# Causal attention: order of whole-array units and maxima on TensorE

## The reference

```python
x = x + attn(layernorm(x), Wq, Wk, Wv)

q = einsum('bte,hed->bhtd', x, Wq); k = ...Wk; v = ...Wv
scores = einsum('bhtd,bhsd->bhts', q, k)
scores = where(causal, scores, -inf) / sqrt(256)
w = softmax(scores, axis=-1)
out = einsum('bhts,bhsd->bhtd', w, v)
```

## Time and profile before

| what | value |
|---|---|
| median of 3 runs | 4440.13 us (4440.07 to 4441.22) |
| span of the profiled execution | 4440.5 us |
| TensorE matmul busy | 4192.7 us, 94% |
| VectorE busy | 2790.9 us, 63% |
| ScalarE busy | 2654.5 us, 60% |
| GpSimd busy | 1452.8 us, 33% |
| maxima, reduction L648 | 738.3 us in 1280 instructions |

### The profile page before, as it was taken

One profiled execution on the slowest core, in us unless ns is written; L12 is line 12 of the kernel. 1 busy time (PEld: TensorE's weight loads), 2 busy tenths in 40 slices (PEclk: granted clock), 3 DMA queues, 4 the chain that ended last, 5 costly groups with the idle time before them and its releaser, 6 DMA issues. The chain is left out here.

```text
span 4440.5 us, 62548 instructions
## 1 busy us (share of the span) xinstructions
PE 4192.7 (94%) x22580; PEld 2203.7 (50%) x22580; DVE 2790.9 (63%) x5566; ACT 2654.5 (60%) x3193; POOL 1452.8 (33%) x1111
## 2 busy tenths in 40 slices
PE   7999999999978999999999999998899999999999
PEld 4444444544535565565565565555344444444443
DVE  6777777777748677676676645554455554555553
ACT  2555555555556454454454423444688888888888
POOL 3111111111125343343343322221354544545545
PEclk7999999999999999999999999999899999999999
DMA  7333433433210000000000001000766667667673
GB/s 176 89 94 74 102 74 81 95 96 80 60 56 1 0 1 1 1 1 1 1 1 1 1 8 26 1 1 1 166 143 161 152 143 164 149 153 162 141 162 90
DMA packets 145746, 322.79 MB, mean 73 GB/s; under 512 B 39296, under 2 KB 64272, under 8 KB 129056
## 3 DMA queue, kind: packets, MB, share of 16 engines
q1 hardware_dynamic: 137456, 310.88, 30.5%
q10 hardware_dynamic: 7920, 7.87, 0.6%
q0 software_dynamic: 64, 0.05, 0.0%
HBM read 237.93 MB, written 80.74 MB: 72 GB/s over the span
## 5 line engine op out<-in xcount | busy, mean ns | idle before, releaser
L2108 ACT ACTIVATE gelu_out<-hidden,b_col 128x1024 f32<-128x1024 f32 x1024 | 1084.4, 1112 | 164.6 <-PE hidden L2008 163.8
L648 DVE TENSOR_REDUCE maxima<-front 128x1 f32<-128x512 f32 (+3 forms) x1280 | 738.3, 631 | 170.7 <-PE front L458 97.2
L2090 POOL TENSOR_TENSOR combined<-combined,gated 128x512 f32<-128x512 f32 x480 | 619.6, 1291 | 666.9 <-DVE gated L2205 458.9
L550 ACT ACTIVATE probsT<-scoresT 128x1024 f32<-128x1024 f32 (+3 forms) x768 | 584.1, 811 | 306.1 <-PE scoresT L486 301.6
L1061 POOL TENSOR_TENSOR pair_sums<-sims 128x1024 f32<-128x1024 f32 x256 | 481.9, 1903 | 784.5 <-DVEq L1187 516.7
L2205 DVE SCALAR_TENSOR_TENSOR gated<-expert_out,b_col,gates_spread 128x512 f32<-128x512 f32 x480 | 360.1, 750 | 501.9 <-PE expert_out L2018 296.2
L2008 PE MATMUL hidden<-slice_stack,w_stack 128*128 128x512 f32 x2048 | 628.0, 428 | 15.0 <-ACT gelu_out L2108 15.0
L2018 PE MATMUL expert_out<-gelu_out,w_sb 128*32 128x512 f32 x4096 | 548.6, 608 | 24.9 <-DVE gated L2205 13.5
L2008 PEld LDWEIGHTS hidden<-slice_stack,w_stack 128*128 128x128 f32 x2048 | 352.4, 189 | 371.8 <-ACT gelu_out L2108 283.1
L399 POOL TENSOR_SCALAR_AFFINE_SELECT probsT<-probsT 128x512 f32<-128x512 f32 x256 | 163.3, 638 | 1075.4 <-ACT probsT L550 1075.4
L452 PE MATMUL front<-k_stack,q_stack 62*128 62x512 f32 (+3 forms) x1536 | 434.8, 427 | 34.6 <-DVE maxima L648 14.7
(11 more groups left out here) (203 smaller groups left out, 5663.0 us busy)
## 6 DMA issues: line engine op xcount, KB each, us to landing
gates_spread<-gate_scratch SPq DMA_DIRECT2D x512, 256.0 KB, 4.9
stack_scratch<-split_parts SPq DMA_DIRECT2D x192, 256.0 KB, 3.0
slice_stack<-slice_scratch SPq DMA_DIRECT2D x128, 256.0 KB, 8.1
q_stack<-stack_scratch SPq DMA_DIRECT2D x64, 384.0 KB, 6.2
k_stack<-stack_scratch SPq DMA_DIRECT2D x64, 384.0 KB, 9.2
slice_scratch<-slice_parts SPq DMA_DIRECT2D x32, 512.0 KB, 6.4
out_x<-x_tiles ACTq DMA_DIRECT2D x15, 512.0 KB, 4.8
x_tiles<-in_L_attn_x SPq DMA_DIRECT2D x7, 1024.0 KB, 12.3
```

What stands on the lines that cost most here:

```text
L550: nc.scalar.activation(PT[:, i % NPT, 2 * pr:2 * pr + 2, at:BANK], ST[pr][:, :, at:BANK], ACT.Exp, scale=SCALE).then_inc(probs_ready, 1)
L648: nc.vector.tensor_reduce(dst, F[k % 3][:, 0:parts * w].rearrange("p (a k) -> p a k", a=parts), AX.X, ALU.max)\
L2090: nc.gpsimd.tensor_tensor(CM[:, par, hc, :], CM[:, par, hc, :], Y[:, u % 2, :], ALU.add)\
L2108: nc.scalar.activation(GH[:, k % 4, :, :], HP[k % HPB][:, :, :], ACT.Gelu, bias=b1c[:, u % E:u % E + 1])\
```

## The change

The planner's second half is rewritten. Whole-array units that come due are no longer put in at once: they are collected in `late` and put in directly behind the next value piece (or the output transpose behind it), where the next piece is a score piece. Pairs of maxima are put in only where the next piece is a score piece, that is between the two score pieces of a group, or behind the value piece, its output transpose and the whole-array units; not ahead of a value piece. The transposes of the row maxima (`turn_after`) are collected in the same way. The load that is caught up with is computed as before, and the number and content of the units are the same.

```diff
-        whole = sum(pe_time(u) for u in pieces if u[0] in "sv")
-        rest, spent = [], 0.0
-        for u in pieces:
-            while spread and spread[0][0] * whole <= spent:
-                rest.append(spread.pop(0)[1])
-            rest.append(u)
-            if u[0] in "sv":
-                spent += pe_time(u)
-        rest += [u for _, u in spread]
-
...
-        whole, spent = sum(load_of(u) for u in rest), 0.0
-        all_pairs, done, k = sum(pair_load(p) for p in pairs), 0.0, 0
-        out = []
-        for u in rest:
+
+        out, late, k = [], [], 0
+        whole, at_whole = sum(pe_time(u) for u in pieces if u[0] in "sv"), 0.0
+        work = sum(load_of(u) for u in pieces) + sum(load_of(u) for _, u in spread)
+        all_pairs, done, spent = sum(pair_load(p) for p in pairs), 0.0, 0.0
+        for u, after in zip(pieces, pieces[1:] + [None]):
             out.append(u)
             spent += load_of(u)
-            while k < len(pairs) and (done + pair_load(pairs[k]) / 2) * whole <= spent * all_pairs:
-                out += pairs[k]
-                done += pair_load(pairs[k])
-                k += 1
-                out += [turn_after[k]] if k in turn_after else []
-        return out + [u for pair in pairs[k:] for u in pair]
+            at_whole += pe_time(u) if u[0] in "sv" else 0.0
+            if u[0] in "vo" and (after is None or after[0] == "s"):
+                while spread and spread[0][0] * whole <= at_whole:
+                    late.append(spread.pop(0)[1])
+                out += late
+                spent += sum(load_of(w) for w in late)
+                late = []
+            if after is None or after[0] == "s":
+                while k < len(pairs) and (done + pair_load(pairs[k]) / 2) * work <= spent * all_pairs:
+                    out += pairs[k]
+                    done += pair_load(pairs[k])
+                    k += 1
+                    late += [turn_after[k]] if k in turn_after else []
+        return out + late + [u for _, u in spread] + [u for pair in pairs[k:] for u in pair]
```

## The result

| | before | after |
|---|---|---|
| median | 4440.68 us (4440.07 to 4442.83) | 4618.66 us (4611.4 to 4634.23) |
| ratio | 1 | 1.0406, 95% interval 1.0387 to 1.0424 |
| span of the profiled execution | 4440.5 us | 4609.7 us |
| last value piece starts | 1279.3 us | 1451.9 us |

A forecast was written before the change was run, and what follows sets the result against it. The prediction took TensorE's own stream plus stalls from tile-form changes and three front banks emptied by VectorE as the bound. Terms -34 - 7 + 88 + 20 + 8 + 17 = +92 us gave 4532 us; range 4460 to 4600.

The forecast's parts named there:

- 1, fewer fragments: Attention on TensorE: 170 fewer row-tiled fragments save 34 us, 64 fewer whole-array ones save 7 us.
- Term 2: Attention's maxima: bunched pairs stall TensorE on three front banks VectorE must empty; +88 us, bounds +45 and +125.
- Term 3: Evacuations losing cover: maxima behind projections +20 us (bounds 0 to 30), o x x x +8 us (0 to 15).
- Term 4: Attention: idle stretches drop TensorE's clock to 1.2 GHz; 7 falls of 2.5 us, +17 us, bounds 0 and +78.
- the third rival: Attention: the clock falls at every long bunch of maxima pairs, +153 us in all, 4593 us; chance 0.11.
- The first (banks don't bind): Attention: fragments are saved and the front banks don't bind, so the kernel gets faster, 4399 us; chance 0.12.
- The second (later waits absorb earlier ones): Attention: TensorE's later waits absorb earlier ones, stalls grow by half, 88 becomes 44, about 4471 us; chance 0.12.
- the clock rival: Same as the third rival: the clock falls at every long bunch in attention, 4593 us; chance 0.11.

The follow-up runs named there:

- e7: Kernel after, with maxima matmuls of second and later pairs in fragments of three or more pairs issued three times; 4594.72 us, 1.0348 of before.
- e12: Kernel before with two front banks in use instead of three; 4753.09 us by one execution.
- e4: Kernel after with VectorE's reduction reading only the first 64 columns of each part; 4436.52 us, 0.9982 of before.
- e5: Kernel before with VectorE's reduction reading only the first 64 columns of each part; 4349.54 us, 0.9792 of before.

## Why the prediction was right or wrong

Step by step, from the trace of the kernel after, with fragments outside the half-clock stretches for the stalls:

| term | forecast | measured |
|---|---|---|
| 1, fewer fragments | -34 and -7 | -34 by the packed prices, not measured by itself; whole-array ones with term 3 about 0 |
| 2, stalls of bunched pairs, and 3, behind p | +88 and +20 | +138 |
| 3, o x x x | +8 | +8 to 15, cancels the -7 |
| 4, clock | +17 | +65 |
| sum | +92 | about +170 (172.6 by the last value piece) |

*What bounds, and the fragments.* Right. At the full clock a value piece takes 1.00 us whatever stands behind it, before and after, and two wide scores alone take 0.66 in both, as packed. No experiment shows the saving by itself, since none saved fragments and left the maxima alone.

*Term 2.* The mechanism and the unit price hold: M M s s behind a value piece stalls 1.00 us at the full clock (54 fragments; forecast 0.95), behind a lone projection 1.82 (forecast 0.95 + 0.8), M s M s 0.87 in the median (forecast 0.85). Mis-sized by 30 us together were the tails: M s M s has a mean of 1.03; three pairs stall 1.9 and not 1.2, since seven of the fifteen stand behind o t w, whose statistics and row-maxima parts are ahead of the reductions in VectorE's queue (2.85 us); and the fragments with one pair stall 0.18 and those with none 0.35 instead of 0.1, so that having fewer of them saved next to nothing. I priced each fragment as though it met an idle VectorE.

*Term 3.* The six places o x x x wait 1.7 to 4.3 us each for normalised x, 14.0 us in all, where I had 1.2 each. About half of the stall was there before in another form: x x o took 2.0 us and x x 1.3 us, six times each, where x x takes 0.59 when nothing holds it up.

*Term 4* is the step that failed most: the number of falls, not their price. I took 7 falls of 2.5 us; there were 29 against 3, and 65 us for 26 more is again 2.5 us each. It is seen best in the value pieces, which wait for nothing once they start: 375 of them took 324 us, where 374 took 303 before, so some 21 us are clock alone, and by the same comparison whole-array fragments give some 26 and row-tiled ones 18. In the prediction the third rival held what was missing as a size (every long bunch brings a fall: +78), with a chance of 0.11. As a mechanism it was half right: 13 of the 29 falls stand behind one of the 32 long bunches of the stage, and behind the others none came within 3.4 us. What I held against it, that the idle stretches are shorter than 1.35 us, didn't help: the longest idle stretch in the window from 641.0 us was 0.90 us. Falls also came where I hadn't looked: 10 of the 29 behind fragments with only two pairs, most of them behind a projection or on the narrow diagonal, and 4 behind o x x x; the last 2 are among the scores at the end of the stage. That these others are set off in the same way is likely but wasn't tested; e7 filled only the long bunches.

*Rivals.* The first (banks don't bind) is refuted by the result, by e12 and by e4 and e5. The second (later waits absorb earlier ones) didn't happen except that scores wait less on the exponentials, 31.6 instead of 68.0 us. The rule of the Trainium skill, TensorEngine Tiling (Array Packing), Key Properties, that a change of tiling mode drains the engine, comes into play some 230 times less here. The 0.2 us of a row-tiled fragment agree with it, though no run separates the drain from the first weight load. The rule of the same page, PSUM Bottleneck, that tiling doesn't speed up the emptying of PSUM, is the one that decided: VectorE's 0.68 us for each reduction is what e4 took away.

The range ended at 4600, the time is 4619. It took in the clock rival only up to 4600 and never that rival together with the upper bound of term 2 (+125), though both have the same cause: longer bunches stall more and let the clock fall more. Ends of terms with one cause belong together.

## What to carry to other kernels

Where several units share a few PSUM banks, what a reorder costs is read from one fragment: how soon the bank comes back (here 1.2 to 1.4 us, of which the reduction is 0.55 to 0.68) and what else TensorE has to do in that time; grouping work of one form to save switches (0.2 us each) takes that cover away. Price each stall by what stands ahead of it in the emptying engine's queue, not from idle. And stalls of a microsecond have a second price: count the stretches in which TensorE idles off and on, since each may bring some microseconds at 1.2 GHz.

## What the runs showed of the hardware

- The granted clock fell to 0.50, the 1.2 GHz level, at 644.4 us behind a stretch in which TensorE was still busy 2.37 of 3.40 us, and at 968.7 us behind one with 3.15 of 3.40; the kernel before showed it behind a wait of 1.35 us. It came back after 3.4 or 6.8 us in 26 of the 29 falls, but in two only after 20.5 us, though TensorE was busy 20.4 of them both times.
- A microsecond at half clock costs some 0.4 us here (an estimate from e7: 89 us less for 32 us, and from the terms: 150 us more for 65 us). A value piece by itself loses nearly half of its time at that level (1.93 us against 1.06); that waits for VectorE take the rest is likely, not shown.
- 524 more matmuls made a kernel 24 us faster.
- A reduction over 64 columns takes 0.22 us and one over 512 takes 0.68, and the bank comes back sooner by all of it: 0.92 against 1.38 us from the first to the fourth unit, behind a first pair of the same width. The other 0.70 us of the way are the same in both.
